# Residual rows and bias accumulated in the output projection's PSUM bank

## What is computed

```python
def reference(...):
    x = L0_attn_x
    x = x + _L0_attn_ref(_layernorm(x), W_qkv, b_qkv, W_out, b_out)   # ends with: out @ W_out + b_out
    x = x + _L0_ffn_ref(_layernorm(x), gate_w, w1, b1, w2, b2, gamma, beta)
    return x
```

## Time and profile before

| | us |
|---|---|
| median of 3 runs | 971.73 |
| the runs | 963.93 to 974.81 |
| profiled execution | 968.54 |
| its span in the profile | 966.7 |
| TensorE, VectorE, ScalarE, GpSimd busy | 845.1, 727.1, 587.1, 466.3 |

### The profile page before, as it was taken

One profiled execution on the slowest core, in us unless ns is written; L12 is line 12 of the kernel. 1 busy time (PEld: TensorE's weight loads), 2 busy tenths in 40 slices (PEclk: granted clock), 3 DMA queues, 4 the chain that ended last, 5 costly groups with the idle time before them and its releaser, 6 DMA issues.

```text
span 966.7 us, 21226 instructions
## 1 busy us (share of the span) xinstructions
PE 845.1 (87%) x6870; PEld 567.3 (59%) x6870; DVE 727.1 (75%) x1658; ACT 587.1 (61%) x1079; POOL 466.3 (48%) x565
## 2 busy tenths in 40 slices
PE   4899977868888978787787899999999999999996
PEld 3455523323343525242242689889888988889875
DVE  6677878876759797988986588786776776666664
ACT  1676557655768787876868464665545554455453
POOL 4000023324435676756486657774476554445441
PEclk9899978777697979899897999999999999999999
DMA  9788658654766868566734751442323332332321
GB/s 203 226 290 281 215 153 234 204 127 125 192 190 205 211 174 213 155 191 175 203 110 136 234 138 27 68 96 49 47 45 53 53 56 45 51 50 47 42 50 18
DMA packets 146327, 130.09 MB, mean 135 GB/s; under 512 B 59344, under 2 KB 128848, under 8 KB 146096
## 3 DMA queue, kind: packets, MB, share of 16 engines
q1 hardware_dynamic: 115648, 87.51, 32.5%
q0 software_dynamic: 15680, 18.95, 12.4%
q10 hardware_dynamic: 14896, 22.28, 7.1%
HBM read 83.63 MB, written 44.80 MB: 133 GB/s over the span
## 4 chain that ended last, share of the span: by engine, by line
PE 40%; DVE 15%; DMA 13%; issue 11%; POOL 10%; SPq 6%; ACT 3%; POOLq 1%; ACTq 0%; DVEq 0%
PE banks L770 12%; PE banks L788 11%; PE banks L583 5%; POOL out L1704 4%; DMA weighed_values<-arena 3%; POOL slot_tokens L1651 3%; PE banks L686 2%; DVE arena L1231 2%; POOL arena L1680 2%; DVE weights L1385 2%; PE banks L573 2%; PE banks L698 2%; PE banks L642 2%; SPq L1782 2%; DMA inverse_sums<-arena 2%
## 5 line engine op out<-in xcount | busy, mean ns | idle before, releaser
L992 ACT ACTIVATE arena<-banks,arena 128x256 f32<-128x256 f32 (+1 forms) x312 | 152.5, 541 | 172.4 <-issue 125.5
L770 PE MATMUL banks<-arena,weights 128*128 128x256 f16 (+1 forms) x1872 | 204.4, 265 | 3.0 <-DVE arena L1487 2.4
L788 PE MATMUL banks<-weights,arena 128*128 x1704 | 193.8, 273 | 0.5 <-DVE arena L1515 0.5
L770 PEld LDWEIGHTS banks<-arena,weights 128*128 x1872 | 173.9, 98 | 28.5 <-issue 4.9
L1704 POOL DMA_INDIRECT out<-arena x71 | 116.2, 1636 | 150.1 <-DVE arena L1526 111.9
L788 PEld LDWEIGHTS banks<-weights,arena 128*128 128x128 f16 x1704 | 165.6, 98 | 20.5 <-issue 1.3
L642 PE MATMUL banks<-arena 64*128 64x128 f16 (+3 forms) x512 | 120.7, 336 | 35.6 <-DMA arena<-arena 12.6
L614 PE MATMUL banks<-arena 62*128 62x384 f16 (+3 forms) x512 | 97.6, 332 | 36.1 <-DVE arena L1228 10.6
L1513 DVE TENSOR_SCALAR arena<-arena 128x512 f16<-128x512 f32 (+1 forms) x156 | 76.2, 489 | 60.4 <-ACT arena L992 58.8
L1515 DVE SCALAR_TENSOR_TENSOR arena<-arena 128x512 f16<-128x512 f32 (+1 forms) x156 | 110.1, 706 | 5.6
L642 PEld LDWEIGHTS banks<-arena 64*128 64x128 f16 x512 | 38.6, 100 | 118.4 <-issue 37.8
(11 more groups left out here) (191 smaller groups left out, 1333.9 us busy)
## 6 DMA issues: line engine op xcount, KB each, us to landing
weights<-in_L_ffn_w ACTq DMA_DIRECT2D x16, 1024.0 KB, 7.7
arena<-in_L_ffn_w SPq DMA_DIRECT2D x32, 512.0 KB, 4.4
qk_parts<-weights SPq DMA_DIRECT2D x64, 128.0 KB
arena<-qk_parts SPq DMA_DIRECT2D x128, 64.0 KB, 3.4
weighed_values<-arena SPq DMA_DIRECT2D x32, 256.0 KB
token_rows<-arena SPq DMA_DIRECT2D x12, 512.0 KB, 5.0
arena<-qk_parts SPq DMA_DIRECT2D x128, 32.0 KB, 3.6
arena<-weighed_values SPq DMA_DIRECT2D x32, 128.0 KB
```

The source lines that it names most:

```text
L770: m = pe.matmul(bank[:, c * TILE:c * TILE + WIDTH[j]], w1[:, k, wp, f:f + P], xp[:, k, 0:WIDTH[j]], start=(i == 0), stop=(i == len(terms) ...
L788: m = pe.matmul(bank[:, c * D:(c + 1) * D], hp[:, f, c * P:(c + 1) * P], w2[:, f // (FC // 2), wp, f % (FC // 2), :], start=(f == 0 and i ...
L992: m = act.activation(h_32[r % 2][:, c, 0:WIDTH[j]], banks[:, 1 + c2, c * TILE:c * TILE + WIDTH[j]], ACT.Gelu, bias=b1_now[j % 2][:, 2 * c2 ...
```

## The change

The two additions to `x2` are gone. TensorE adds the rows of x in the projection's own bank, as a matmul of the unit matrix with `x2`, and the bias, as a matmul of three rows of ones with three rows that hold the bias in bfloat16 parts (the first part, the rest's first part, and the rest of that). ScalarE copies the bank over `x2`.

```diff
-            at(base + 186, "with_bias", b)
-                at(base + 193 + 12 * half, "add_out", (b, half))
...
             def out_proj(b, half):
                 w.wait_ge(sem("o_divided"), KC * (b + 1))
                 w.wait_ge(sem("vectors_in"), 96)
+                w.wait_ge(sem("bias_parts_in"), 48)
+                w.wait_ge(sem("x_again"), 16 * (b + 1))
                 bank = take_side("out_proj", (b, half))
                 for s in range(2):
                     tt = 2 * half + s
+                    out = bank[:, s * D:(s + 1) * D]
                     for k in range(KC):
-                        m = pe.matmul(bank[:, s * D:(s + 1) * D], o_inverse[k][:, tt * P:(tt + 1) * P], w_out[:, k, :],
-                                      start=(k == 0), stop=(k == KC - 1))
+                        pe.matmul(out, o_inverse[k][:, tt * P:(tt + 1) * P], w_out[:, k, :], start=(k == 0), stop=False)
+                    pe.matmul(out, ident, x2[:, tt, :], start=False, stop=False)
+                    m = pe.matmul(out, ones_b[0:3, :], b_out[0:3, :], start=False, stop=True)
...
             def copy_x(b, k):
-                w.wait_ge(sem("out_added"), KC * b + k + 1)
+                if b > 0:
+                    w.wait_ge(sem("side_made"), side_made("gate", b - 1))
...
             def copy_out(b, half):
                 w.wait_ge(sem("side_made"), side_made("out_proj", (b, half)))
-                if b > 0:
-                    w.wait_ge(sem("side_made"), side_made("gate", b - 1))
-                act.copy(turned[:, half, :], side_bank("out_proj", (b, half))).then_inc(sem("act_freed"), 1)
+                act.copy(x2[:, 2 * half:2 * half + 2, :],
+                         side_bank("out_proj", (b, half)).rearrange("p (s d) -> p s d", s=2)).then_inc(
+                    sem("act_freed"), 1)
...
             def moments_of(b, tt):
-                w.wait_ge(sem("out_added"), KC * b + tt // 2 + 1)
+                w.wait_ge(*side_out("out_proj", (b, tt // 2)))
...
             m.then_inc(sem("memory_set"), 1)
+
+            w.wait_ge(sem("vectors_in"), 96)
+            m = own.mark(g.tensor_copy(bias_part[0], bias_all))
+            w.wait_ge(own.sem, m)
+            m = own.mark(g.tensor_tensor(bias_rest[0], bias_all, bias_part[0], ALU.subtract))
+            w.wait_ge(own.sem, m)
+            m = own.mark(g.tensor_copy(bias_part[1], bias_rest[0]))
+            w.wait_ge(own.sem, m)
+            m = own.mark(g.tensor_tensor(bias_rest[1], bias_rest[0], bias_part[1], ALU.subtract))
+            w.wait_ge(own.sem, m)
+            m = own.mark(g.tensor_copy(bias_part[2], bias_rest[1]))
+            w.wait_ge(own.sem, m)
+            for i in range(3):
+                g.dma_start(b_out[i:i + 1, :], bias_part[i][i:i + 1, :]).then_inc(sem("bias_parts_in"), 16)
```

More of the change, by code:

```diff
@@ L141, in build @@
         banks = ctx.enter_context(nc.psum_tensor("banks", [P, 8, 512], F32))
-        keep = Area(arena, 0, 3088)
+        keep = Area(arena, 0, 3088 + D // 2)
         ident = keep.take(P)
@@ L152, in build @@
         beta = keep.take(D)
-        b_out = keep.take(D)
+        scratch = keep.take(D)
+        b_out = keep.take(D // 2, BF16)
         w_out = keep.take(KC * D, k=KC, n=D)
@@ L242, in build @@
         b_v = a1.take(D)
+        bias_all = p_T[1][:, 0, 0:D]
+        bias_rest = [p_T[1][:, 0, (1 + i) * D:(2 + i) * D] for i in range(2)]
+        bias_part = [p_T[1][:, 0, 3 * D + i * D // 2:3 * D + (i + 1) * D // 2].bitcast(BF16) for i in range(3)]
         qk_full = [a1.take(T) for _ in range(2)]
@@ L1076, in numbers @@
                 w.wait_ge(sem("consts"), 1)
-                v.tensor_copy(iota_16, b_out[:, 0:P].bitcast(I32))
+                v.tensor_copy(iota_16, scratch[:, 0:P].bitcast(I32))
                 v.memset(running, 0.0)
-                v.tensor_copy(prefer, b_out[:, P:P + E].bitcast(I32)).then_inc(sem("numbers"), 1)
+                v.tensor_copy(prefer, scratch[:, P:P + E].bitcast(I32)).then_inc(sem("numbers"), 1)
             def rsqrt_step(step, s, y_, u_):
@@ L1241, in invert @@
                 v.reciprocal(sums[u % 2], sums[u % 2]).then_inc(sem("inverted"), 1)
-            def add_out(b, half):
-                w.wait_ge(sem("with_bias"), b + 1)
-                w.wait_ge(*side_out("out_proj", (b, half)))
-                own_x = x2[:, 2 * half:2 * half + 2, :]
-                v.tensor_tensor(own_x, turned[:, half, :].rearrange("p (s d) -> p s d", s=2), own_x,
-                                ALU.add).then_inc(sem("out_added"), 1)
             norm_at = [0]
             def moments_of(b, tt):
-                w.wait_ge(sem("out_added"), KC * b + tt // 2 + 1)
+                w.wait_ge(*side_out("out_proj", (b, tt // 2)))
                 norm_at[0] = own.mark(v.bn_stats(moments[:, tt, :], x2[:, tt, :]))
@@ L1558, in vector @@
                     low_weights(n)
-                elif stage == "add_out":
-                    add_out(*n)
                 elif stage == "moments":
@@ L1610, in gpsimd @@
                             channel_multiplier=-1)
-            g.iota(b_out[:, 0:P].bitcast(I32), [[1, P]], base=0, channel_multiplier=0)
-            g.iota(b_out[:, P:P + E].bitcast(I32), [[-1, E]], base=E, channel_multiplier=0)
+            g.iota(scratch[:, 0:P].bitcast(I32), [[1, P]], base=0, channel_multiplier=0)
+            g.iota(scratch[:, P:P + E].bitcast(I32), [[-1, E]], base=E, channel_multiplier=0)
             g.iota(spare_row, [[0, LOCAL]], base=N, channel_multiplier=1)
@@ L1717, in gpsimd @@
                     place(*n)
-                elif stage == "with_bias":
-                    w.wait_ge(sem("x_again"), 16 * (n + 1))
-                    w.wait_ge(sem("vectors_in"), 96)
-                    g.tensor_tensor(x2, x2, over_tiles(b_out), ALU.add).then_inc(sem("with_bias"), 1)
                 elif stage == "gamma" and n < B - 2:
```

2 lines of the change are left out of this document (1 added, 1 removed).

## The result

The changed kernel takes 989.25 us (median of 4 runs, 988.23 to 990.34), the kernel before 969.26 us in the same comparison: a ratio of 1.0201, with a 95% interval from 1.0162 to 1.0239. By the ratio it is 19.5 us slower (the medians differ by 20.0). The forecast was 982 us, so the way was right and the size was not: the sum said +11.6.

What follows compares the result with a forecast made beforehand. TensorE was taken to bound the expert stage and, at each projection, to keep the attention stage's other engines waiting. Terms of 10.6 - 1.3 + 1.8 + 0.5 = +11.6 us led to a forecast of 982 us, range 967 to 994.

Steps and rivals of the forecast that it cites:

- The bias product: Output projection on TensorE: each three-row bf16 product of 256 columns takes 0.11 us, bounds 0 to 0.22.
- The unit matrix: Output projection on TensorE: each added f32 product with the unit matrix takes 0.45 us, two in a half.
- The clock surcharge: Attention stage: two halves run at 1.2 instead of 2.4 GHz, so their added matmul time doubles, +2.2 us.
- the clock rival: Stalls for x lower TensorE's clock: 996 us, chance 0.10; sign: attention stage grows over 20 us, clock below 0.85.
- The wait: TensorE's first projection matmul waits for the reloaded x in batches 1 to 4: +4.2 us, bounds 0 and 8.
- VectorE -4.4: Attention stage: of VectorE's removed additions only each batch's second counts, 6 x 0.73 = -4.4 us, bounds 0 and -8.8.
- A quarter absorbed: Attention stage: a quarter of the +14.1 us is absorbed in TensorE's idle time, leaving +10.6 us.
- The seam: Batch 6, before the expert stage: two TensorE waits go, -3.55 us, against +2.24 of new matmuls, -1.3 us.
- Batch 7: In the full expert stage: +2.24 us of matmuls, -0.48 for a wait on GpSimd's division, +1.8 us.
- The start: Kernel start: GpSimd's split of the bias may collide with VectorE's scale computation, +0.5 us, bounds 0 and 2.7.
- VectorE as the bound: Rival: VectorE bounds the attention stage, the matmuls go into TensorE's idle time: -10.1 us, 962 us, chance 0.11.
- Half hidden: Rival: the reload issues early enough and half of the 15.6 us falls in idle time: +3.1, 975 us, chance 0.27.

Runs made afterwards that it cites:

- run 2: The changed kernel without the unit-matrix and bias matmuls, the wait for x moved from TensorE to ScalarE's copy: 0.9891 of the kernel before, -10.6 us.
- run 3: The changed kernel without the unit-matrix and bias matmuls, TensorE's wait for x kept: 0.9958 of the kernel before, -4.1 us.
- run 4: The changed kernel without the bias matmul alone: 1.0067 of the kernel before, +6.5 us.
- run 5: The changed kernel with a bias matmul of all 128 rows, 125 of them zeros: 1.0086 of the kernel before, +8.3 us.
- run 6: The changed kernel with a bias matmul of 64 rows, 61 of them zeros: 1.0176 of the kernel before, +17.1 us.
- wait_only: The kernel before with one line added, TensorE's output projection waiting for the reloaded x: 1.0059 of the kernel before, +5.7 us.
- run 11: The kernel before with GpSimd's add of the bias to x cut to 8 columns of one block: 0.9965 of the kernel before, -3.4 us.
- run 7: The changed kernel with each half's eight matmuls grouped by kind, w_out, unit matrix, then bias: 1.016 of the kernel before, +15.5 us.
- run 9: The changed kernel with one unit-matrix and one 128-row bias matmul of 512 columns per half, both and the wait for x behind w_out: 1.003, +2.9 us.

## Why the prediction was right, and where its size was off

The parts, by differences of the runs: relief -10.6 (run 2), wait +6.5 (run 3 less run 2), unit matrix +10.6 (run 4 less 3), bias +13.0 (the changed kernel less run 4); together +19.5. They add up by construction, each being the step from one kernel to the next, so the sum by itself proves nothing. The differences are uncertain by some 4 to 7 us each; that the small bias product is dear rests on runs 4, 5 and 6, whose intervals stand clear.

By the same parts the prediction had: matmuls +20.1 (17.9 for 16 halves and 2.2 for the clock), wait +4.2, relief -9.7, start +0.5, absorbed -3.5. Against 23.6, 6.5, -10.6, nothing and little, the miss of 7.9 us is 3.5 in the matmuls, 2.3 in the wait and 3.5 in the absorption, less 0.9 and 0.5. Inside the matmuls a bias product 9.5 us too cheap was partly made good by a unit matrix 3.8 us too dear and a clock surcharge of 2.2. That the forecast came within 7.3 us owes something to luck.

- **The bias product, "I take 0.11".** This is the term that was mis-sized most. 32 x 0.11 = 3.5 us plus a surcharge for the clock were counted and 13.0 measured. The bounds, 0 to 0.22 by the duration of an f32 instruction, were bounds of the instruction itself; both left out what it does to its neighbours, and the measured 0.41 is above the upper one. "The same column count" was a fair guide for 128 rows (run 5 shows 0.11) and none for three. A hint lay in the trace of before: a load of 128 rows behind loads of 62 has an idle time there as well. I had not looked at the loads. In the kernel before, the load that stands directly ahead of batch 4's projection, behind scores of 62 rows:

```profile
429.85 0.11 PEld L627 LDWEIGHTS banks<-arena 128*128 128x128 f16 x2 [0.21 <-issue]
```

- **The unit matrix, 0.45 each.** 32 of them are 14.4 us; 10.6 were measured. At full clock run 4's piece shows 0.43. Where the rest went is not shown; the difference is within the uncertainty of 4 us.
- **The clock surcharge, +2.2.** Taken for two halves. In the changed kernel more are at the lower clock: batch 0's first (0.51), both of batch 1 (0.79 and 0.72 in the windows around them), both of batch 2 (0.50 and 0.72), batch 4's first (0.55). Only batch 2's first and batch 4's stand right behind a wait for x; batch 0's stands behind GpSimd's division, as before. No run sizes this term.
- **The sign for the clock rival.** The prediction said that it was the clock if the stage grew by over 20 us and the clock fell below 0.85. To the letter that came: 22.0 us, and 0.84 where it had been 0.85. The sign was set too near to the value of before. Over whole executions the changed kernel's four runs had 0.924 to 0.936, mean 0.932, while the 19 runs of the kernel before beside runs 1 to 4 had a mean of 0.924. With the granted clock as the mean of two levels, 1 and 0.5, that is about 135 us at the lower level in the changed kernel and 148 before (an estimate, 2 x (1 - clock) x span). More time at the lower clock is not what made it slower. In wait_only (mean 0.921) the same estimate gives 153 us, 6 more, of which at most half is lost time.
- **The wait, 4.2 (bounds 0 to 8).** 5.7 and 6.5 by two ways; the stalls seen are 6.7 us in four batches of the changed kernel. Right in kind, and the batches were 2 to 5 and not 1 to 4. A later TensorE didn't find its rows there, because the reload comes later too: by the code it waits for the batch before. In batch 4 TensorE was ready 12.6 us later than before (442.53 instead of 429.97), the reload was issued 15.0 us later (439.61 instead of 424.66). The rule on the clock that the prediction cites from the Trainium skill (TensorE: Matmul & The Clock Gate, HAM oscillation — how this bites in real kernels) is borne out in two of the four batches that wait for x: the clock granted behind the stalls of 2.13 and 3.40 us was 0.50 and 0.55, behind those of 0.78 and 0.38 it was 1.00.
- **VectorE -4.4, the gate's wait -1.3, the seam's waits -3.55, and -0.48 in batch 7.** Together -9.7 for the relief; -10.6 measured (-17 to -4). GpSimd's add alone gives 3.4, which includes the seam. "In each batch the first lies in a gap" was read from batch 4 alone: in batch 3 of before the next maximum follows the first addition with no idle time (385.06 for 0.62, then 385.79).
- **"A quarter absorbed", -3.5.** Little sign of it. At full clock 16 halves of 1.6 us are 25.6 us, and 23.6 (uncertain by 5) reached the end. The attention stage grew by 22.0 us (from batch 0's projection, -2.2, to batch 6's, +19.8) where 10.6 were summed. The bias accounts for most of the difference: 12 of its 16 halves lie there, so 13.0 x 12/16 = 9.8 us where 12 x 0.22 = 2.6 were counted, a difference of 7.1. The prediction's 14.1 before absorption plus 7.1 are 21.2 us, near the 22.0, and nothing need be absorbed. This is a reckoning; no run tests the absorption by itself.
- **The seam, -1.3.** From batch 6's projection to batch 7's the two timelines differ by -0.95 us (19.8 to 18.85). Right: GpSimd stands before no wait of TensorE there, and the first expert matmul waits 0.41 us for VectorE instead of 1.43.
- **Batch 7, +1.8.** +3.05 us (18.85 to 21.9): two halves of 1.6 us each, where TensorE is full. The same mis-sized term again.
- **The start, +0.5.** The first scaled copy waits until 25.25 us, have 25.45: nothing. GpSimd's first cast came at 22.91, the rest from 30.44 on. One VectorE step beside that cast took 0.27 us instead of 0.17 (23.05 to 23.32) and ended with it (23.31): a hold of 0.1 us. The row at 17.01 that the prediction leans on is of another kind, an instruction with one input beside memsets that read nothing, so it is no instance of the rule for two inputs.

Of the rivals, VectorE as the bound had the size of the relief right (-10.6 without the matmuls), but not what it said of them: they did not go into TensorE's idle time, since 23.6 us of them reached the end. VectorE waited longer for TensorE behind the projection of batch 3, 5.41 us where the same batch had 3.91 before, which is about the 1.6 us by which the half grew. Before, then the changed kernel:

```profile
382.24 0.96 DVE L1233 TENSOR_REDUCE arena<-banks 128x2 f32<-128x768 f32 x1 [3.91 <-PE banks L627]
396.34 0.96 DVE L1241 TENSOR_REDUCE arena<-banks 128x2 f32<-128x768 f32 x1 [5.41 <-PE banks L629]
```

Batch 4, whose 2.36 us the prediction expected to become 3.4, waits 8.60, the stall of 3.40 and the lower clock included. "Half hidden" falls by the same 23.6 us. The stall with its clock is real and smaller than its rival's 14 us. What stays open is how the 6.5 us of the wait divide into stall and clock (no run holds the clock apart), what the clock surcharge of the added matmuls was, and how the relief divides between VectorE, ScalarE's hop and GpSimd beyond the third of run 11.

The Trainium skill (TensorE: Matmul & The Clock Gate, The mechanism) says that a weight load is pulled ahead of matmuls in flight when it goes to other row groups or to the background buffer, and lists as seen in traces that it overlaps only when the row group differs. This case's traces don't fit the "only": loads with the same 128 rows as the matmul in flight ran ahead of their own matmul (385.82 against 386.03 in run 5), which the background buffer would allow, and the ones of 3 and 64 rows did not (0.33 us "issue"). The same page of the Trainium skill (Step-by-step: what each phase is for) says that the number of rows doesn't matter for a load; for its duration the rows agree (92, 94 and 105 ns for 3, 64 and 128), for what it costs they do not: 11 us over this kernel between 3 and 128 rows.

## What to carry to other kernels

A matmul with fewer rows than its 128-row neighbours broke the run of weight loads here: its load waited for the matmul in flight and the next load began only with its own matmul, some 0.3 us a time. Padding it with zero rows took that away (run 5); putting its kind together left one gap for two (run 7), but the time didn't tell. Read PEld beside PE, because PE's rows spread this cost over the neighbours. When an operand is moved onto the engine that sets the pace, the wait for that operand moves with it: put the products that don't need it first (run 9, where no wait for x was left). A copy that frees a bank early can be worth more than the add it duplicates.

## What was not expected of the hardware

- Adding 125 rows of zeros to a product of three rows made the kernel 11 us faster (+19.5 to +8.3 us); 64 rows (+17.1) were not told apart from three.
- The gap before such a load grows with the matmul ahead of it: 0.33 us behind 256 columns in fp32, 0.76 behind 512.
- A stall of 2.02 us in wait_only was followed by a granted clock of 0.50 in the window from 436 to 442 us; one of 0.78 in the changed kernel left it at 1.00 from 390 to 393 us.
